# GpSimd arithmetic moved to VectorE and ScalarE in a one-core graph, attention and expert layer; head 0's maxima first; the first two units of sums held in used token space

## What is computed

```python
xn = _layernorm(x)
# graph part: two attention layers over 20000 edges and 1250 loops, 4 heads of 192, then 2 heads of 96
e = leaky_relu(s_src[src] + s_dst[dst], 0.2)
ee = exp(e - segment_max(e, dst)[dst])
out = segment_sum(ee / segment_sum(ee, dst)[dst] * h[src], dst) + bias
# mixer part: random-feature attention with 12 heads
x = x + concat(xn, out2) @ Wu + bu + mix(xn)
# experts: softmax over 8 logits of the normalised x, top 2, weights shared out by balance
x = x + sum_of_two(gate * (silu(y @ w1[e].T) @ w2[e].T))
```

## Time and profile before

| | us |
|---|---|
| median of 3 runs | 1039.6 |
| the profiled execution | 1039.45 |
| its span | 1037.7 |
| PE busy | 926.1 (89%) |
| DVE busy | 633.2 (61%) |
| POOL busy | 447.5 (43%) |
| ACT busy | 383.8 (37%) |

### The profile page before, as it was taken

The page is one execution under the profiler, slowest core; times in us unless marked ns, Lnnn a source line. Parts: engine busy times, 40 slices in busy tenths (PEclk is TensorE's granted clock), DMA queues, the critical chain, the costliest instruction groups (busy, mean ns, idle before and its releaser), DMA issues.

```text
span 1037.7 us, 14087 instructions
## 1 busy us (share of the span) xinstructions
PE 926.1 (89%) x5131; PEld 790.7 (76%) x5131; DVE 633.2 (61%) x1215; ACT 383.8 (37%) x575; POOL 447.5 (43%) x331
## 2 busy tenths in 40 slices
PE   3899699999999999999789899998778659999994
PEld 2798586686768799999779789987777657777673
DVE  7655996802056532269789999888996773222221
ACT  2534240104333300045576666544973512111110
POOL 3028888888888888012010000010000224666664
PEclk9899899969999999999899999999988869999998
DMA  9995479434225446840120020042403934777775
GB/s 315 212 158 108 61 168 320 91 25 68 1 1 122 61 75 203 189 155 1 51 103 23 1 52 1 1 153 71 143 1 118 377 139 72 130 130 127 123 122 61
DMA packets 84850, 112.44 MB, mean 108 GB/s; under 512 B 37980, under 2 KB 63821, under 8 KB 84783
## 3 DMA queue, kind: packets, MB, share of 16 engines
q0 software_dynamic: 39120, 39.85, 25.5%
q1 hardware_dynamic: 43357, 65.40, 20.4%
q10 hardware_dynamic: 2306, 6.29, 1.6%
HBM read 80.02 MB, written 31.49 MB: 107 GB/s over the span
## 4 chain that ended last, share of the span: by engine, by line
PE 51%; DVE 27%; DMA 8%; issue 7%; ACT 3%; POOL 2%; SPq 1%; POOLq 0%; DVEq 0%; ACTq 0%
PE bank L1665 41%; DVE sb_before L1344 7%; PE bank L1930 6%; DVE pbuf L1440 5%; DVE pbuf L1414 4%; DMA ygot<-y_d,fetch 4%; PE bank L1676 2%; DVE junk_k L1218 2%; DMA keyrow<-key_d 2%; DVE h L1423 2%; POOL out L748 1%; DMA out<-orow,send 1%; ACT vbuf L1027 1%; SPq L552 1%; DVE o L1423 1%
## 5 line engine op out<-in xcount | busy, mean ns | idle before, releaser
L665 POOL DMA_INDIRECT table<-match_n,slot_ix x168 | 277.3, 1651 | 96.8 <-issue 48.3
L1930 PE MATMUL bank<-h,pbuf 128*128 128x197 f32 (+1 forms) x1200 | 193.3, 321 | 27.9 <-DVE pbuf L1440 27.3
L1930 PEld LDWEIGHTS bank<-h,pbuf 128*128 128x128 f32 x1200 | 184.0, 196 | 37.1 <-DVE pbuf L1440 34.8
L748 POOL DMA_INDIRECT out<-orow,send x54 | 84.6, 1568 | 59.4 <-DVE orow L1650 49.2
L1344 DVE CUSTOM_DVE_ANT_0 sb_before<-a_row,pen 128x1280 bf16<-128x1280 f32 x60 | 101.2, 1686 | 14.2 <-ACT pen L979 8.0
L1218 DVE SCALAR_TENSOR_TENSOR junk_k<-keyrow,key,sb_before 128x384 uint8<-128x384 f32 x168 | 92.8, 614 | 26.2 <-DMA keyrow<-key_d 26.1
L1650 DVE TENSOR_SCALAR orow<-bank,gates 128x384 f32<-128x384 f32 x54 | 33.4, 618 | 111.5 <-PE bank L1665 98.7
L1036 ACT ACTIVATE pbuf<-pbuf 128x1280 f32<-128x1280 f32 x60 | 76.2, 1270 | 62.8 <-DVE pbuf L1414 62.8
L1665 PE MATMUL bank<-xnT_hi,w_hi 128*128 128x512 f32 (+1 forms) x216 | 86.4, 400 | 4.4 <-DVE xnT_lo L1142 3.5
L1440 DVE SCALAR_TENSOR_TENSOR pbuf<-pbuf,cnt 128x1280 f32<-128x1280 f32 x60 | 88.7, 1485 | 0.0
L1665 PE MATMUL bank<-w_hi,xnT_hi 128*128 128x384 f32 x240 | 83.1, 346 | 0.0
(11 more groups left out here) (351 smaller groups left out, 1674.8 us busy)
## 6 DMA issues: line engine op xcount, KB each, us to landing
keyrow<-key_d SPq DMA_DIRECT2D x28, 384.0 KB
cnt<-table POOLq DMA_DIRECT2D x20, 320.0 KB, 9.2
f_all<-in_w1T SPq DMA_DIRECT2D x8, 768.0 KB, 9.2
f_all<-in_w2T SPq DMA_DIRECT2D x8, 768.0 KB, 10.9
u_row<-m_d POOLq DMA_DIRECT2D x8, 640.0 KB, 5.9
w_raw<-in_kqvT SPq DMA_DIRECT2D x4, 1152.0 KB
acc_d<-ubuf SPq DMA_DIRECT2D x20, 192.0 KB, 2.5
x<-acc_d SPq DMA_DIRECT2D x10, 384.0 KB, 6.4
```

The costliest lines, as they stand in the source:

```text
L665: pool.indirect_dma_start(table[i], bass.IndirectOffsetOnAxis(ap=slot_ix[:, g:g + 1], axis=0), match_n[:, g:g + 1], None, compute_op=ALU.a ...
L748: pool.indirect_dma_start(half_rows, bass.IndirectOffsetOnAxis(ap=send[:, hf, a:a + 1], axis=0), orow[a % 3][:, hf * HALF:(hf + 1) * HALF] ...
L1930: ins = nc.tensor.matmul(b[:, d * stride:d * stride + v.shape[-1]], score[:, dt * P:(dt + 1) * P], v, start=st == 0 and d == 0, stop=st == ...
```

## The change

- **GpSimd.** The gain and split of the second W1 half go to VectorE (`split_gain_lo` after mask tile 2). The split of `wuo` goes to VectorE, after the last unit of the second attention. The ten `yrow` tiles go to ScalarE (`normal_rows`), and SP sends them.
- **Maxima.** Mask tiles are made one `h1` tile earlier. For tiles 4 to 9 VectorE does head 0 first; heads 1 and 2 follow. TensorE turns head 0's row after tile (1, 3) instead of (1, 5). The row of head 2 leaves through SP, as that of head 3 already did. The rows of the layer's biases are summed ahead of tile 4.
- **First two units.** Their branches and weights stand in `ahead`, the columns of `xnT` that `h1` no longer needs, as 5 pieces of 256. So ScalarE starts them after tiles (1, 7) and (1, 8). The 40 idle transposes are gone.
- **Sums.** ScalarE copies head 0's five banks out, scaled; VectorE only takes the reciprocals. Of the last head VectorE first takes the 4 score columns of each tile, then starts the next stage, then takes the other 192 columns, and only these free the banks.
- **Second attention.** ScalarE writes its first two leaky branches inside the router's stage. `fin` waits for each output bank by itself.
- **Choice.** Constants are made inside `fin`; the pick works on the logits and no longer waits for the probabilities.

```diff
-        rec = sb("rec", [P, 5])
+        rec = sb("rec", [P, NT])
-        a_row = [at(f"a_row{h}", 92960 + 5120 * h if h < 3 else TAIL, [P, T]) for h in range(H1)]
+        a_row = [at(f"a_row{h}", (98080, 103200, 92960, TAIL)[h], [P, T]) for h in range(H1)]
+        ahead = at("ahead", 0, [P, KD, T])
+        AHEAD = 2
+        def weights_of(g):
+            return ahead[:, 0:5, 512 * g + 256:512 * g + 512] if g < AHEAD else in_fives(pbuf[g % 3][:, :])
-        PEN_AT = {(0, 2): [0], (0, 3): [1], (0, 4): [2], (0, 6): [3], (1, 0): [4, 5], (1, 1): [6, 7], (1, 2): [8, 9]}
-        ROWS_AT = {(1, 5): 0, (1, 6): 1, (1, 8): 2}
+        PEN_AT = {(0, 1): [0], (0, 2): [1], (0, 3): [2], (0, 4): [3], (0, 9): [4, 5], (1, 0): [6, 7], (1, 1): [8, 9]}
+        ROWS_AT = {(1, 3): 0, (1, 6): 1}
...
@@ gpsimd
-            nc.gpsimd.tensor_tensor(w_raw[i][:, :, :], w_raw[i][:, :, :], gain, ALU.mult).then_inc(gain_done, 1)
-            ins = nc.gpsimd.tensor_tensor(w_lo[i][:, :, :], w_raw[i][:, :, :], w_hi[i][:, :, :].bitcast(F32), ALU.subtract)
+                if h == 0:
+                    pool.wait_ge(max_done, HEADS_01)
                     pool.dma_start(u1_row[0][:, :], row_of(m_d, 0)).then_inc(u_row_in[0], 16)
...
-            nc.gpsimd.tensor_tensor(wuo_lo[:, :, :], wuo_raw[:, :, :], wuo_hi[:, :, :].bitcast(F32), ALU.subtract)
-                nc.gpsimd.tensor_scalar(yrow[t % 4][:, :], x1[:, t, :], lgs[:, t, E:E + 1], rs2[:, t:t + 1], ALU.add, ALU.mult)
@@ scalar
+                    if (hf, t) == (1, 7):
+                        first_leak(0)
+                    if (hf, t) == (1, 8):
+                        first_leak(1)
+                        first_exp(0)
...
+                        for d in range(2):
+                            ins = nc.scalar.activation(h2_rows[:, 2 * k + d, :], pv[:, d, 0:SO], ACT.Copy, scale=rec[:, 2 * k + d:2 * k + d + 1])
+                        ins.then_inc(free("agg", 0, k), 1)
...
+                if t in (SPREAD_AT + 2, SPREAD_AT + 3):
+                    second_leak(t - SPREAD_AT - 2)
...
+                nc.scalar.activation(yrow[t % 4][:, :], x1[:, t, :], ACT.Identity, scale=rs2[:, t:t + 1],
+                                     bias=a02[:, 0, t:t + 1]).then_inc(y_done, 1)
@@ vector
+                if dt == 2:
+                    split_gain_lo(dve, A0 + 1)
+            bias_of_layer()
...
+            for k in range(5):
+                b = finished(dve, "agg", H1 - 1, k)
+                step(nc.vector.reciprocal(...))
+                last_head(k, slice(C2, S2), False)
...
+            for k in range(5):
+                last_head(k, slice(0, C2), True)
+                evacuated(dve, "agg", H1 - 1, k)
...
+                if i == H2 * NT - 1:
+                    dve.wait_ge(g_hi_done, 1)
+                    nc.vector.tensor_tensor(wuo_lo[:, :, :], wuo_raw[:, :, :], wuo_hi[:, :, :].bitcast(F32), ALU.subtract)
@@ tensor
-            keep_running(("agg", 0, 0), 40)
-            evacuated_all(pe, "agg2")
+                if t in (0, 5):
+                    evacuated(pe, "agg2", H2 - 1, t // 5)
```

More of the change, by code:

```diff
@@ L613, in _ @@
                 sp.dma_start(out[t * P:t * P + rows(t), :], x1[0:rows(t), t, :]).then_inc(out_sent, 16)
+            for t in range(NT):
+                sp.wait_ge(y_done, t + 1)
+                sp.dma_start(y_d[t * P:(t + 1) * P, :], yrow[t % 4][:, :]).then_inc(y_out[t % 4], 16)
             sp.wait_ge(out_sent, 16 * NT)
@@ L1362, in max_row_out, with all_maxima @@
+            bias_of_layer()
+            def all_maxima():
+                dve.wait_ge(max_done, maxima[0])
             def max_row_out(h):
                 b = finished(dve, "mT", h)
-                if h >= 2:
-                    dve.wait_ge(m_out[h - 2], 16)
-                nc.vector.tensor_copy(mrow[h % 2][:, :], b[0:2 * NT, 0:P]).then_inc(free("mT", h), 1)
-            for dt in range(4, NT):
-                evacuated(dve, "pen", dt, 0), evacuated(dve, "pen", dt, 1)
-                masked_max(pen[dt], a_row, (0, 1), dt)
@@ L1371, in _, with head_maxima @@
-            dve.wait_ge(max_done, NT)
-            leaky_max(H1, 0, 1), leaky_max(H1, 1, 1)
-            for dt in range(4, NT):
-                if dt == 7:
-                    max_row_out(0), max_row_out(1)
-                masked_max(pen[dt], a_row, (2,), dt)
-            dve.wait_ge(max_done, NT + NT - 4)
-            leaky_max(H1, 2, 1)
+                nc.vector.tensor_copy(mrow[h][:, :], b[0:2 * NT, 0:P]).then_inc(free("mT", h), 1)
+            def head_maxima(h, tiles):
+                for dt in tiles:
+                    evacuated(dve, "pen", dt, 0), evacuated(dve, "pen", dt, 1)
+                    masked_max(pen[dt], a_row, (h,), dt)
@@ new lines, in last_head @@
+            def last_head(k, cols, last):
+                pv = psum("agg", H1 - 1, k)[:, 0:2 * S1].rearrange("p (d c) -> p d c", d=2)
+                for d in range(2):
+                    t = 2 * k + d
+                    ins = nc.vector.scalar_tensor_tensor(
+                        out=h2[:, t, :, cols], in0=pv[:, d, 0:SO].rearrange("p (e c) -> p e c", e=H2)[:, :, cols], scalar=rec[:, t:t + 1],
+                        in1=h2[:, t, :, cols], op0=ALU.mult, op1=ALU.add)
+                    ins.then_inc(free("agg", H1 - 1, k), 1) if last and d else step(ins)
```

255 lines of the change are left out of this document (145 added, 110 removed).

## The result

The changed kernel took 1009.68 us in the median (1007.48 to 1012.44, four runs), the kernel before 1039.35 us (1037.38 to 1040.23, four runs). The ratio is 0.9718 with a 95% interval of [0.9691, 0.9746], which makes 29.3 us less, between 26.4 and 32.1. Forecast were 1014.0 us and 25.4 us less. A second set of runs gave 1007.32 against 1035.89 us, a ratio of 0.9737 [0.9707, 0.9766], which is 27.2 us.

The account below looks back on a forecast made before the run. The chain of waits was half TensorE and a quarter VectorE, neither bounding alone, which left the seams. The terms -13.8 + 0.8 - 4.2 - 1.5 - 6.7 summed to -25.4 us, or 1014.0, range 1007 to 1023.

Parts of the forecast that it names:

- A: Start of the first attention: unit 0 begins at 512.0 instead of 525.82, gain 13.8 us (7.2 to 15).
- R1: Rival at the first attention's start: head 0's shift is late and TensorE stalls again, 1020.6 us; chance 0.15.
- B: Head 0 to head 1: ScalarE falls short by 1.0 us and VectorE waits, +0.8 us (-3 to +4).
- The copies' part: Head 0 to head 1: ScalarE gets ten copies of 192 columns, about 0.4 us each, so 4.0 us.
- C: Between the attentions: the second attention's unit 0 starts at 723.9 instead of 728.08, -4.2 us (gain 1 to 7).
- first maximum later by 1.0: Second attention's first maximum: later than 684.61 by about five long sums less a 3.24 us wait, +1.0 us.
- D: Output projection: TensorE starts behind the first bank, the `wuo` split fits VectorE's idle time; -1.5 us (0 to -2.5).
- E: The choice: without GpSimd beside VectorE, `full_of` starts at 830.15; -6.7 us (-7.5 to -3).
- R3: The clock rival: TensorE stays at half rate from unit 0, 3.6 us per unit, eight give 1043 us; chance 0.03.
- R4: Rival: the stretched VectorE instructions are not GpSimd's doing, 1029 us; chance 0.03.

Follow-up runs that it names:

- second set of runs: The changed kernel again, unaltered, against the kernel before: 1007.32 us, 0.9737 [0.9707, 0.9766].
- whole sums: Changed kernel with the last head's sums divided out whole, ahead of the score columns: single timed execution 1003.66 us, stretch between the attentions 107.73 us.
- the pause filled: Changed kernel with whole sums, Silu table load behind the `yrow` tiles and nine idle transposes ahead of the new rows: 1003.94 us, 0.9698 [0.9677, 0.9719].

## Why the prediction was right

- **A, 13.8 us forecast, 13.66 measured.** Step by step it went as worked out: the maxima start 3.1 us earlier, the shift meets the end of tile (1, 3) (a margin of 0.6 was forecast, a stall of 0.27 is left), the row is there when ScalarE comes to the first branch, unit 0 follows. The three experiments on it take away what they should: 5.65 us with the split on GpSimd, 4.97 with the branches not woven in, and 1.35, over A and B together, with the transposes back. R1 did not come about, though by little; with the split on GpSimd its event does, a stall of 4.36 us and 5.65 us lost, where its price was 6.6.
- **B, 0.8 us slower forecast, 0.63 faster measured.** The copies' part is right in sign and mostly in size (0.54). What was missed is the clock at the start. The first three units take 12.16 us from start to start instead of 12.66; in the kernel before they ran at a mean clock of 0.86 behind its long pause, in the changed one at 1.00. I had noted the 1.2 us that the clock cost there and not booked its return. The rest of the miss lies in the switch to head 1: from unit 10 to unit 15 it takes 22.07 us instead of 22.20, where the forecast had it 0.8 longer. Why it is no slower in spite of the 0.54, no run here shows.
- **C, 4.2 us forecast; 3.4 and 1.7 at unit 0, 4.0 and 4.3 at the stage's end.** That the sum is near is in part luck, by two errors against each other. The term "first maximum later by 1.0" measured 2.9 and 4.5 us (12.22 and 13.81 against 9.28). It was worked out from waits for banks alone; to these came the low clock, 0.78 and 0.63. In the first profile the rows' spread starts 1.6 us later than before (7.67 against 6.06 us behind the first of the last sums) and takes 6.05 instead of 4.73 us. Against it stands that the wait for the branch and the slow spread ahead of unit 0 gave more than the 2.05 us that I had left for them. The end of C agrees in both profiles because a slow unit 0 in the one met a slow clock inside the second attention in the other. That the last head's split sums earn nothing was not in the forecast; by the one profile of each, whole sums are better by 1 us, and by 3 with the pause filled.
- **D, 1.5 forecast, 1.6 and 0.1 measured**, by the clock in the output projection. The start went as forecast in both (the transposes begin 4.32 us behind the last product instead of 6.57); the rest is which clock TensorE then gets, and the forecast had no term for it. Nine of the thirteen profiles with the change have 34.0 us, four 35.5.
- **E, 6.7 forecast, 6.8 measured**, 5.6 us of it GpSimd's; the 1.2 left over come with the shorter pick. The fetch was forecast to be hidden by 1.7 us and is 0.57 us late: the tiles take 0.94 us each (3.77 for four), not 0.82, and the last one's transfer lands only 1.27 us ahead of the fetch.
- **R3, the clock rival, and R4.** The half clock did not come at unit 0, which was its place and price. It did come elsewhere: at the new rows and at the output projection, as the tables of windows show, within the second attention, and in the first profile also from 559.70 to 563.10 (0.50, where the second has 1.00). There it cost nothing, since B is 148.88 us in both profiles. In the second attention the kernel before had it as well, 0.50 from 769.50 to 779.70. Where it was paid for was the new rows and the projection: the forecast priced the clock at nothing for unit 0, rightly, and had no term for these two. R4 is refuted by three kernels in which GpSimd's instructions, put back one at a time, bring the stretches back.
- **The total.** 25.4 us were forecast for the touched part, and 26.1 and 24.9 measured. The timed gain of 29.3 and 27.2 us is larger. The interval of the second set reaches down below the stretches' sum (24.2 against 24.9 us); that of the first ends just above it (26.4 against 26.1). In the profiles the surplus lies ahead of the touched part (439.06 us in the one profile of the kernel before, 429.78 to 437.41 with the change) and in the expert stage (190.69 against 187.46 to 189.72). With one profile of the kernel before I can't say whether that is chance or an effect that the forecast lacks. For chance speaks that the profiled execution took 1039.45 us, while the medians of the kernel before in the later sets of runs were 1034.94 to 1036.65 us; for an effect, that all thirteen profiles with the change lie below it in both places. It stays open.

## What to carry to other kernels

Read what GpSimd's large instructions do to VectorE's durations beside them before counting GpSimd's time as free: here 8.4, 3.1 and 5.6 us of VectorE's hung on three pieces of such work, and most of it lay on the path. When an edit removes a wait of VectorE's, look at TensorE's pauses next to it; a pause of a microsecond or two can cost as much again in clock. Filling it with idle work is worth a trial when the work fits in it; ahead of unit 0, where it did not fit, it lost 1.35 us. And judge edits of 1 to 3 us by the lengths of stretches between fixed instructions, since those repeat to some 0.05 us where no clock or DMA comes in, while the whole time moves by several. Where the clock comes in, as in C, even a stretch moves by 2 us between kernels that do not differ there, so one profile is not enough.
